# Sorted experts in a 12-block decoder: routing order, an unrolled tile loop, and the queue of the next block's weights

## What is computed

```python
# L2_ffn, second half ("l2fm"): one expert for each token
hn2 = layernorm(x, ln2_g, ln2_b)
idx = argmax(hn2 @ gate_w + gate_b)                       # 8 experts
y_e = relu(hn2 @ w1[e] + b1[e]) @ w2[e] + b2[e]           # 256 -> 1024 -> 256
x = x + y_idx
# L3_ffn ("l3f"): two experts for each token, the last sub-layer
score = relu(xf @ rw1 + rb1) @ rw2 + rb2
gate = softmax over the two best scores
out = sum over the two experts of gate_e * (relu(xf @ W1[e] + b1[e]) @ W2[e] + b2[e])
```

## Time and profile before

| | |
|---|---|
| median of three runs | 3135.05 us |
| the profiled execution's own time | 3131.25 us |
| its span, first to last instruction | 3129.5 us |
| mean granted TensorE clock | 0.92 of full speed |
| PE / DVE / ACT / POOL busy | 84% / 59% / 39% / 25% |
| l2fm: routing, tiles, combine | about 51, 202 and 19 us |
| l3f: routing, tiles, combine | about 105, 326 and 25 us |

### The profile page before, as it was taken

One profiled execution on the slowest core, in us unless ns is written; L12 is line 12 of the kernel. 1 busy time (PEld: TensorE's weight loads), 2 busy tenths in 40 slices (PEclk: granted clock), 3 DMA queues, 4 the chain that ended last, 5 costly groups with the idle time before them and its releaser, 6 DMA issues. The chain is left out here.

```text
span 3129.5 us, 46962 instructions
## 1 busy us (share of the span) xinstructions
PE 2637.7 (84%) x15124; PEld 1819.2 (58%) x15125; DVE 1832.2 (59%) x3997; ACT 1209.2 (39%) x3068; POOL 791.6 (25%) x613
## 2 busy tenths in 40 slices
PE   3998989899688785899989979869969687869996
PEld 1565766666455453677766757646645465446664
DVE  6884986488788445343444659843355588333334
ACT  2223654166677222344334436511212566212221
POOL 4433530144100132222222236421110233121110
PEclk8999999999787798999999999979989898989998
DMA  9001000000200323000000020140020300431113
GB/s 303 1 1 47 13 16 3 14 1 1 62 4 1 88 93 122 28 1 1 1 24 25 11 68 2 41 164 30 29 72 1 86 11 1 153 106 32 32 32 99
DMA packets 158960, 142.40 MB, mean 46 GB/s; under 512 B 59012, under 2 KB 146068, under 8 KB 158388
## 3 DMA queue, kind: packets, MB, share of 16 engines
q1 hardware_dynamic: 145828, 111.95, 12.5%
q0 software_dynamic: 8688, 23.82, 2.1%
q10 hardware_dynamic: 4256, 4.20, 0.4%
HBM read 97.12 MB, written 42.81 MB: 45 GB/s over the span
## 5 line engine op out<-in xcount | busy, mean ns | idle before, releaser
L873 POOL TENSOR_TENSOR room<-room 128x1024 f32<-128x1024 f32 x144 | 273.1, 1897 | 458.9 <-DVE room L818 458.6
L812 DVE TENSOR_REDUCE room<-room 128x8 f32<-128x1024 f32 x144 | 174.0, 1208 | 0.0
L1312 PE MATMUL l3f_hidden<-room,Y 128*128 x312 | 145.6, 610 | 1.2 <-DVE Y L1552 0.6
L1331 PE MATMUL l3f_out<-room,Y 128*128 x624 | 141.1, 379 | 1.6 <-DVE Y L1577 1.6
L549 PE MATMUL l2a_proj<-room 128*128 128x256 f32 x512 | 128.2, 399 | 14.3 <-ACT room L896 14.3
L1331 PEld LDWEIGHTS l3f_out<-room,Y 128*128 128x128 f32 x624 | 118.5, 190 | 34.1 <-issue 20.0
L873 POOL TENSOR_TENSOR room<-room,l2a_rinv 128x1024 f32<-128x1024 f32 x32 | 60.7, 1896 | 253.5 <-DVE l2a_rinv L818 253.5
L549 PEld LDWEIGHTS l2a_proj<-room 128*128 128x128 f32 x512 | 97.1, 197 | 32.0 <-issue 17.0
L1688 POOL DMA_INDIRECT results<-Y,l3f_dest x39 | 37.2, 955 | 296.6 <-DVE Y L1585 161.3
L942 ACT ACTIVATE room<-l2a_scores,l2a_nmx 128x128 f32<-128x128 f32 x256 | 72.3, 381 | 93.6 <-DVE l2a_nmx L804 93.6
L1659 ACT ACTIVATE Y<-l3f_hiddenT,vecs 128x128 f32<-128x128 f32 x156 | 44.6, 368 | 157.5 <-PE l3f_hiddenT L1322 157.5
(11 more groups left out here) (749 smaller groups left out, 6732.3 us busy)
## 6 DMA issues: line engine op xcount, KB each, us to landing
sorted_rows<-zeros SPq DMA_DIRECT2D x1, 16512.0 KB, 67.5
room<-in_L_ffn_w SPq DMA_DIRECT2D x16, 1024.0 KB, 12.4
room<-in_L_ffn_W SPq DMA_DIRECT2D x16, 1024.0 KB, 12.2
Y<-sorted_rows SPq DMA_DIRECT2D x62, 129.0 KB, 2.1
room<-in_ctx SPq DMA_DIRECT2D x24, 256.0 KB, 2.7
room<-results SPq DMA_DIRECT2D x12, 512.0 KB, 7.4
room<-sorted_rows SPq DMA_DIRECT2D x39, 129.0 KB, 2.1
Y<-results SPq DMA_DIRECT2D x8, 512.0 KB, 5.9
```

The costliest lines, as they stand in the source:

```text
L812: dve.tensor_reduce(rsum[:, u % 2, :], p[:, u % (TURN + 1), :, :], AX.X, ALU.add)
L873: pool.tensor_tensor(p[:, u % (TURN + 1), :, :], p[:, u % (TURN + 1), :, :], rinv[:, u % (TURN + 1), :].unsqueeze(2).to_broadcast([P, HEAD ...
L1312: mm = pe.matmul(hbank[a][:, :], rowsT[:, par, kc, :], chip.room[:, bass.ds(at + (kc * F + a * half_f), half_f)], start=(kc == 0), stop=(k ...
L1331: mm = pe.matmul(obank[par][:, 0:D], hT[:, f, :], chip.room[:, bass.ds(at + (SLOT // 2 + f * D), D)], start=(f == 0), stop=(f == HC - 1))
```

## The change

1. Flat router (l2fm): each group is taken from its turning to its scatters before the next; DVE normalises a group (`normalise(g+1)`) just before it chooses for group g, adds Y to X a group at a time before `send`, and ACT empties both halves of `yT`.
2. Both routers: DVE's block starts with the first group's normalising, without the `sem_inc`s; in the deep router `empty_yT(0)` comes before the other groups' normalising.
3. The tile loop is written out: no loop instructions, constants in waits and addresses, `LEAD` and two marker semaphores gone, one load of the weights' address for a tile on PE instead of two.
4. The next block's weights are sent from ACT's queue as soon as the last tile's second layer is filled, ahead of the last result scatter and of the reading back; before it ACT loads the table with the root.
5. l2fm finishes its statistics itself (aggregation for each group, then root and reciprocal), and gau finds "rstd".

```diff
@@ tensor
-                    for k in range(NG + 3):
+                    for k in range(NG + 1):
                         if k < NG:
                             turn_rows(k)
-                        if 0 <= k - 1 < NG:
-                            logits_flat(k - 1)
-                        if 0 <= k - 2 < NG:
-                            logits_back(k - 2)
-                        if 0 <= k - 3 < NG:
-                            rank(k - 3)
+                            logits_flat(k)
+                        if k:
+                            rank(k - 1)
+                        if k < NG:
+                            logits_back(k)
...
-                with pe.Fori(0, NT // 2) as i:
-                    step(i, 0)
-                    step(i, 1)
-                turn_hidden(NT // 2, 0)
-                second_layer(NT // 2, 0)
+                for n in range(NT):
+                    after = None
+                    if n + 1 < NT:
+                        after = weights_of(n + 1)
+                        turn(n + 1)
+                    turn_hidden(n)
+                    if n + 1 < NT:
+                        first_layer(n + 1, after)
+                    second_layer(n, at)
+                    at = after
@@ vector
-                for x in (rowsT_ready, h_copied[0], hT_ready[0], out_ready, dest_ready):
-                    dve.sem_inc(x, LEAD)
-                w.wait(dve)
-                ln_stats_vector(chip, dve, src, s, have=have_stats)
-                for b in range(NB):
+                ln_stats_vector(chip, dve, src, s, have=have_stats)
+                def normalise(g):
+                    for b in range(g * GR, (g + 1) * GR):
...
+                normalise(0)
+                w.wait(dve)
...
-                empty_yT(0)
-                if plan.from_y:
-                    dve.tensor_tensor(chip.X[:, :, :], chip.X[:, :, :], chip.Y[:, :, :], ALU.add)
                 if deep:
+                    empty_yT(0)
+                    for g in range(1, NG):
+                        normalise(g)
                     empty_yT(1)
...
-                    for k in range(1, NG + 3):
-                        if k < NG:
-                            empty_yT(k)
-                        if 0 <= k - 1 < NG:
-                            empty_lT(k - 1)
-                        if 0 <= k - 2 < NG:
-                            choose(k - 2)
-                        if 0 <= k - 2 < NG:
-                            send(k - 2)
+                    for g in range(NG):
+                        empty_lT(g)
+                        if g + 1 < NG:
+                            normalise(g + 1)
+                        choose(g)
+                        if plan.from_y:
+                            mine = slice(g * GR, (g + 1) * GR)
+                            dve.tensor_tensor(chip.X[:, mine, :], chip.X[:, mine, :], chip.Y[:, mine, :], ALU.add)
+                        send(g)
...
                         for b in range(g * GR, (g + 1) * GR):
                             dve.bn_stats(chip.bn[:, b, :], chip.X[:, b, :])
-                dve.drain()
+                        dve.drain()
+                        for b in range(g * GR, (g + 1) * GR):
+                            dve.bn_aggr(chip.mv[:, b, :], chip.bn[:, b, :])
+                dve.drain()
+                if not last:
+                    ln_stats_vector(chip, dve, chip.X, final, have="mv")
@@ sync
-                if prefetch:
-                    prefetch.load(sp)
@@ scalar
-                empty_yT(0)
+                if deep:
+                    empty_yT(0, 1)
...
+                    for g in range(NG):
+                        for kc in range(KC):
+                            empty_yT(g, kc)
...
+                for n in range(NT):
+                    relu(n)
+                    if n + 1 < NT:
+                        empty_hidden(n + 1)
+                if prefetch:
+                    act.preload_act_table(ACT.Sqrt)
+                    act.wait_ge(out_filled, NT)
+                    prefetch.load(act)
+                    ln_stats_scalar(chip, act, final)
@@ table of what a block leaves
-"l2fm": "bn"
+"l2fm": "rstd"
```

More of the change, by code:

```diff
@@ L1065, in sorted_experts_block @@
     NT = NB * keep + NE - 1
-    assert NT % 2 == 1 and F == HC * P
+    assert F == HC * P
     half_f = F // 2
@@ L1187, in _ @@
             def _(pe):
-                for x in (turned, *h_filled, *hT_filled, out_filled):
-                    pe.sem_inc(x, LEAD)
                 w.wait(pe)
@@ L1578, in relu, with empty_out @@
                     op.then_inc(hT_ready[0], 1)
[L1580 to L1603 removed]
+                def empty_out(n):
+                    at = dve.value_load(b2_at[0:1, n:n + 1], min_val=0, max_val=(NE - 1) * D)
+                    dve.wait_ge(out_filled, n + 1)
+                    if n >= 2:
+                        dve.wait_ge(returned[n % 2], n // 2 * 16)
+                    dve.tensor_tensor(result[:, n % 2, :], obank[n % 2][:, 0:D], w.v["b2"][:, bass.ds(at, D)], ALU.add).then_inc(out_ready, 1)
+                empty_rows(0)
+                aim(0)
+                empty_hidden(0)
+                for n in range(NT):
+                    if n + 1 < NT:
+                        empty_rows(n + 1)
+                    relu(n)
+                    if n + 1 < NT:
+                        aim(n + 1)
+                        empty_hidden(n + 1)
+                    empty_out(n)
                 for g in range(NG):
@@ L1681, in _ @@
                                                     yn[:, b, :], None).then_inc(scattered, 16)
[L1683 to L1694 removed]
+                for n in range(NT):
+                    pool.wait_ge(dest_ready, n + 1)
+                    pool.wait_ge(out_ready, n + 1)
+                    pool.indirect_dma_start(results[0:keep * TOK + NT * P, :], bass.IndirectOffsetOnAxis(dest[:, n % 2:n % 2 + 1], 0),
+                                            result[:, n % 2, :], None).then_inc(returned[n % 2], 16)
 def routed_block(chip, plan, w, prefetch, have_stats):
@@ L3903 @@
 DOUBLE_LN = {b for b, (_, plan) in PLANS.items() if plan.double_ln}
-LEAVES_STATS = {**{b: "rstd" for b in PLANS}, "rwkv": "rstd", "l1x": "rstd", "l1f": "rstd", "l2fm": "bn", "l0f": "rstd", "gau": "rstd"}
+LEAVES_STATS = {**{b: "rstd" for b in PLANS}, "rwkv": "rstd", "l1x": "rstd", "l1f": "rstd", "l2fm": "rstd", "l0f": "rstd", "gau": "rstd"}
 USES_Y = ("l2fa", "l2fm", "l3f")
```

207 lines of the change are left out of this document (77 added, 130 removed).

## The result

The kernel after took 3141.24 us (median of ten runs, 3139.41 to 3142.82), the kernel before 3135.12 in ten runs on the same chip: ratio 1.0022, 95% interval 1.0013 to 1.0032. That is 6.1 us slower. The forecast was 3138.95 in a range of 3130 to 3147; the time lies in the range, on the side of rival (a). The prediction called +3.9 us "no change that a measurement tells"; the interval, 4.1 to 10.0 us at 3135, lies above that sum and above nothing. The profiled execution took 3142.4 us, its span 3140.6, 11.1 more than the span before.

What follows compares the result with a forecast made beforehand. It took PE to bound l3f's tiles, and a chain through PE, ACT, DVE and POOL, ended by POOL's pace, l2fm's routing. Terms +5.4 -2.05 -1.7 +2.0 +0.25 = +3.9 us gave 3138.95; range 3130 to 3147.

Steps and rivals of the forecast that it cites:

- rival (a): Between 2277 and 2288: weights collide with last scatter and reading back, 6.9 in place of 2.0, total 3143.9; chance 0.25.
- its own sign: In l2fm: the forecast is wrong if routing isn't longer, or if the end takes over 5 us more.
- part 3: Tile loops of l2fm and l3f: writing them out saves 0.06 us in each of 28 iterations, -1.7 us.
- part 1: Routing of l2fm: taking one group after another makes it longer by 5.4 us, bounds -0.6 and +8.0.
- part 4: End of l2fm: early weights delay the last scatter and the reading back, +2.0 us for both.
- part 5: Combine of l2fm and start of gau: finishing the statistics in l2fm costs a net +0.25 us.
- a ring: Routing of l2fm: chain from one group's bias to the next, 11.0 us at low clock, 8.4 at high.
- POOL's pace alone: Routing of l2fm in the kernel before: POOL's scatters, one every 1.27 us, set the stage's end.
- one ring in three: Routing of l2fm: the share of rings given the high clock, which made the term +5.4 us.
- all-low bound: Routing of l2fm with everything at the low clock: it ends at 2081.0 against 2072.99, 8.0 us later.
- The bulk addition: Start of l2fm's routing: removing 4.4 us of DVE in one piece is worth nothing of its own.
- Part 2: Start of l3f: PE starts 1.65 us sooner and DVE 0.4 sooner, -2.05 us, bounds 0 and -2.2.

Runs made afterwards that it cites:

- part 4 alone: The kernel before with only the next block's weights issued early from ACT's queue: 3135.89 us against 3126.62, ratio 1.0027.
- after without part 4: The kernel after with its weights back on SP's queue behind the reading back: 3124.81 us, ratio 0.9994 against the kernel before.
- The staggered kernel: Kernel before with written-out tile loop, shorter starts, ACT emptying both halves of `yT`, X's addition by groups, PE's stagger kept: 3129.62 us, ratio 0.9977.

## Why the prediction was right or wrong

**Right in sign and within the range, but not by its terms, and by its own sign wrong.** It said that the forecast as a whole is wrong if the end of l2fm takes over 5 us more; it took 8.1 more. That the sum still fell in the range owes something to luck: part 3 gained 1.8 us more than forecast and part 1 cost 1.6 less, against 6.1 too little for part 4. The measured stages sum to +7.4 us where +3.9 was forecast. Rival (a) was the one that came about: it was to decide from 4.4 us in its place, and that place took 8.1, over even its upper bound of 6.9.

**Part 4 is the step that failed.** "So 0 to 4.9, and 1.2 by the median; the reading back may then meet the rest of the weights, 0 to 2. I take 2.0 for both." The scatter was delayed 2.9 to 3.7 us (after, and part 4 alone), within its bounds but not near the median. The median of the earlier trace rows was taken under a stream of 1 MB pieces; the rows did not say what four matrices, three wide vectors and nine pieces of small elements do. The reading back lost 4.9 us where 2 was the bound. That bound had no row, and its picture, a reading back that meets the rest of the bytes, isn't what the trace shows: for 4.91 us after its issue it moved nothing, at the end of that with the DMA engines a quarter busy; with the matrices and wide vectors alone it still lost 2.8 (6.74 against 3.92). "DVE, not the DMAs, sets the pace behind the first group" held: the additions of the four groups follow each other every 3.06 to 3.30 us, the same to 0.01 in after and in after without part 4 (2.62 to 2.64 before; part 5's aggregation stands between them), so only the first group's delay counts. The gain on the other side, "an earlier landing gives nothing", held too: gau starts no sooner. The rule cited from the Trainium skill (DMA: Bandwidth & Descriptors, Issuing engines are not separate DMA queues) says that transfers of different engines share the DMA engines and interleave. The runs agree that moving the issue buys nothing and costs: +5.9 us in this stage with part 4 alone, and 7.8 us gone when it is taken back. But sharing alone would have let the reading back move packets between ACT's, and in its first 4 us it moved none.

**Part 1: the mechanism was right, the size too large by 1.6 us** (+3.8 against +5.4; +3.5 between the means of the two groups of kernels above). Each group's scatters wait on a ring, POOL idles between the fours, and the stage ends later; alone it cost 4.5 us in its stage and 3.3 in the whole. The first scatters of the fours lie 9.25, 10.12 and 7.52 us apart; the last is under the 8 to 11 that was forecast, because no further group is turned ahead of its rank. The reading of the kernel before as POOL's pace alone left out the 2.29 us that POOL waited for the second group. Two errors went against each other. The rings at the low clock were 9.77, 9.80 and 10.12 us, not 11.0: the rank comes 0.3 after the logits (0.6 taken), and the handovers cost next to nothing where 0.9 was taken. And the clock stayed at 0.50 all the time, where one ring in three was to be at the high clock. Three rings 1.1 shorter, a first bias 0.4 earlier (8.49 us after the start, against 8.93) and a tail 0.45 shorter (14.15) take 4.2 from the all-low bound of +8.0, which gives the +3.8 measured.

**The bulk addition** "is worth nothing of its own": wrong, as far as the runs part it. POOL's pace sets the end only counted from when it can begin. The staggered kernel without it, and with ACT emptying both halves, sent its first scatter 7.2 us sooner and ended the routing 4.2 us sooner.

**Part 2 held**: l3f's first matmul into its hidden layer came 5.35 us after the block's start (7.65 before), 2.3 nearer, and the routing was 1.64 shorter (2.2 between the means of the kernels without and with it). **Part 3 was twice the forecast**: -1.67 and -1.85 us against -1.7 for both. The alternation is gone as said. From 28 iterations it makes 0.06 each, or 1.7; the other 1.8 is not in DVE's boundary rows, and no run parted it. The rule of the Trainium skill on instruction fetch (Runtime: NRT & Kernel Launch, Instruction fetch mechanics) would have a stall at each taken branch that leaves the two pages held. The loops cost 3.5 us in this pair and 4.1 between the means of four kernels with them and ten without, so 0.13 to 0.15 us for each of 28 iterations, all engines together; no trace here tells a stall from the jump itself. **Part 5** cost 0.4 to 0.85 us in its stage against 0.25.

**The bounds.** The upper bounds of the terms add up to +15.2 (8.0, 0, 0, 6.9, 0.25), not +13, and the range was cut narrower than either bound. The measured time needed neither.

## What to carry to other kernels

A transfer moved to an earlier place on another queue is judged by what it meets there: name the latency-bound transfer that the path waits for, and price the meeting at no less than its upper bound unless a row shows that very mix. Ask also when it would start to move, and not only how many bytes stand before it. In a chain of small steps over several engines, a serial order adds each group's whole ring to the path; keep the stagger, and look instead for long instructions, such as a bulk addition, that stand ahead of the first group. Idle matmuls shortened such a chain in the one kernel where PE waited anyway, and lengthened it in the one where other engines waited for what stood behind them. And hold two kernels against each other stage by stage before a difference of a few microseconds is believed.

## What the runs showed of the hardware

- Sixteen pieces sent from ACT's queue lengthened the time from the last scatter's start to SP's release from 2.42 us to 5.30 (6.16 with that part alone), and the first group's reading back from 3.92 to 8.84.
- A reading back issued from SP's queue moved its first packet 1.05 us after the issue in the kernel before, and 3.50 to 5.34 us after it in the five kernels with the matrices sent from ACT's queue ahead of it (4.91 in after), part of that time with the DMA engines 0.21 to 0.25 busy.
- In 2 us behind the matrices the DMA engines were 0.55 busy and moved 20 GB/s.
- The granted clock was 0.50 over a routing stage with PE busy 25.68 of 52.33 us. With 56 idle matmuls in the same stage, PE busy 24.05 of 46.58, it was 0.76 in the mean, and the stage was 5.75 us shorter.
- An untouched cross-attention block took from 216.5 to 228.3 us in different kernels, with a mean granted clock of 0.91 in the shortest and 0.85 in the longest, and the start of l2fm lay within 14.6 us. A difference of a few microseconds between two spans is only an effect of an edit if the stage with the edit shows it.
